# Cross attention and a mixture of experts on one core: bf16 slot tables, packed expert numbers, and two scatter buffers in turn

## What is computed

```python
logits = h @ router_w                                   # 8 experts, h: 1024 tokens x 128
probs = jax.nn.softmax(logits, axis=-1)
topv, topi = jax.lax.top_k(probs, TOPK)                  # TOPK = 2
topv = topv / jnp.sum(topv, axis=-1, keepdims=True)
weights = jnp.sum(jax.nn.one_hot(topi, E, dtype=h.dtype) * topv[..., None], axis=-2)
gate = jnp.einsum('bsd,edm->bsem', h, w_gate)            # m = 448
up = jnp.einsum('bsd,edm->bsem', h, w_up)
act = jax.nn.silu(gate) * up * weights[..., None]
moe = jnp.einsum('bsem,emd->bsd', act, w_down)
return x + moe
```

## Time and profile before

| | |
|---|---|
| time, median of 3 runs | 635.01 us (633.67 to 635.02) |
| the profiled execution's own time | 633.75 us |
| its span | 631.8 us |
| PE busy | 518.7 us, 82% of the span |
| DVE / ACT / POOL busy | 431.9 / 373.0 / 372.3 us |
| `mixture` begins | 483.6 us after the span's start |

### The profile page before, as it was taken

One profiled execution on the slowest core, in us unless ns is written; L12 is line 12 of the kernel. 1 busy time (PEld: TensorE's weight loads), 2 busy tenths in 40 slices (PEclk: granted clock), 3 DMA queues, 4 the chain that ended last, 5 costly groups with the idle time before them and its releaser, 6 DMA issues. The chain is left out here.

```text
span 631.8 us, 11030 instructions
## 1 busy us (share of the span) xinstructions
PE 518.7 (82%) x3275; PEld 407.3 (64%) x3275; DVE 431.9 (68%) x967; ACT 373.0 (59%) x968; POOL 372.3 (59%) x661
## 2 busy tenths in 40 slices
PE   5899899999899898999988647998986463999920
PEld 4567678777677676787766535665554463899920
DVE  5748877886888687978589526998984440577621
ACT  4548767877667766777677416898883200444400
POOL 1527966776777775787676556366965401565431
PEclk9789999999999999999999866999998555899975
DMA  8200010000100000000000011002220100011103
GB/s 298 66 1 1 2 34 2 1 2 2 35 0 2 2 1 1 1 2 2 2 0 2 2 49 47 2 1 89 88 89 18 33 0 18 29 48 39 35 21 108
DMA packets 17018, 18.49 MB, mean 29 GB/s; under 512 B 3041, under 2 KB 14305, under 8 KB 16961
## 3 DMA queue, kind: packets, MB, share of 16 engines
q1 hardware_dynamic: 15024, 14.71, 7.5%
q0 software_dynamic: 1472, 3.02, 1.5%
q10 hardware_dynamic: 464, 0.07, 0.1%
HBM read 15.23 MB, written 2.56 MB: 28 GB/s over the span
## 5 line engine op out<-in xcount | busy, mean ns | idle before, releaser
L1168 POOL TENSOR_SCALAR attn_probs<-attn_probs,rinv 128x512 f32<-128x512 f32 x128 | 90.4, 719 | 20.4 <-DVE rinv L1025 20.3
L860 ACT ACTIVATE attn_probs<-bank,bias 128x512 f32<-128x512 f32 x128 | 87.3, 687 | 13.6 <-DVE bias L1018 13.6
L1034 DVE TENSOR_TENSOR pT_lo<-bank,pT_hi 128x512 fp32r<-128x512 f32 x128 | 86.8, 680 | 7.4 <-ACT pT_hi L878 5.8
L690 PE MATMUL bank<-ident,attn_probs 128*128 128x128 f32 x512 | 78.4, 282 | 14.0 <-POOL attn_probs L1168 11.3
L1010 DVE TENSOR_REDUCE neg_max<-bank 128x1 f32<-128x512 f32 x128 | 83.9, 676 | 4.0 <-PE bank L673 4.0
L690 PEld LDWEIGHTS bank<-ident,attn_probs 128*128 128x128 f32 x512 | 56.3, 142 | 41.3 <-POOL attn_probs L1168 26.0
L878 ACT ACTIVATE pT_hi<-bank 128x512 fp32r<-128x512 f32 x128 | 74.2, 595 | 8.9 <-PE bank L690 8.0
L722 PE MATMUL bank<-pT_hi,vals 128*128 128x256 f32 x256 | 66.3, 291 | 2.2 <-DVE pT_lo L1034 1.4
L722 PE MATMUL bank<-pT_lo,vals 128*128 128x256 f32 x256 | 64.2, 283 | 0.0
L722 PEld LDWEIGHTS bank<-pT_hi,vals 128*128 128x128 f32 x256 | 48.8, 191 | 4.8 <-DVE pT_lo L1034 2.0
L1161 POOL TENSOR_TENSOR total<-row_sum,e 128x2 f32<-128x2 f32 x64 | 15.0, 234 | 62.3 <-ACT e L867 59.4
(11 more groups left out here) (312 smaller groups left out, 1490.0 us busy)
## 6 DMA issues: line engine op xcount, KB each, us to landing
ctx_raw<-in_ctx_T SPq DMA_DIRECT2D x4, 512.0 KB, 3.5
gu_raw<-in_L_ffn_w_gate SPq DMA_DIRECT2D x4, 448.0 KB, 3.5
gu_raw<-in_L_ffn_w_up SPq DMA_DIRECT2D x4, 448.0 KB, 4.3
wkv_raw<-in_L_xattn_Wkv SPq DMA_DIRECT2D x3, 512.0 KB, 8.9
dn_raw<-in_L_ffn_w_down SPq DMA_DIRECT2D x8, 192.0 KB, 4.2
y_in<-y_rows SPq DMA_DIRECT2D x4, 256.0 KB, 3.7
wkv_raw<-in_L_xattn_Wkv SPq DMA_DIRECT2D x2, 256.0 KB, 6.0
wq_raw<-in_L_xattn_Wq SPq DMA_DIRECT2D x1, 512.0 KB, 6.2
```

The lines of the kernel that those rows point to most:

```text
L690: last = pe.transpose(t_bank[half][:, j * N + t * P:j * N + (t + 1) * P], probs[:, g % 2, i, t, kt * P:(kt + 1) * P], k.ident[:, :])
L860: act.activation(probs[:, g % 2, i, t, :], score_bank(G, i)[:, :], ACT.Exp, bias=bias[:, t, h:h + 1], scale=X_SCALE, accum_out=row_sum[:, ...
L1034: dve.tensor_tensor(pT_lo[:, i, 2 * half:2 * half + 2, :], t_bank[half][:, :].rearrange("p (j n) -> p j n", j=2), f(pT_hi[:, i, 2 * half:2 ...
L1168: pool.tensor_scalar(probs[:, g % 2, i, t, :], probs[:, g % 2, i, t, :], rinv[:, t, h:h + 1], 1.0, ALU.mult, ALU.mult).then_inc(p_norm_s, 1)
```

## The change

The code of the attentions, of `fetch_pair` and of `split_pair` is the same. In `mixture`:

- The tables `chosen`, `in_tile`, `row_in`, `in_lane`, `share_in` become bf16, and so do the constants `earlier`, `ones`, `lanes`, which ACT casts from `slots` into `slots_b` as its first work in the stage. Numbers that bf16 doesn't hold are cut: `row_in` has two columns sets, a group number of 1 to 16 (`turns`) and the partition number (`row`), and a share is cut by POOL into three bf16 parts.
- The expert numbers of 8 tiles are packed into one number in base 8, so that PE reads 3 numbers instead of 23. The number of a tile is got back by a shift and a mask on PE's registers.
- The products of the shares stand behind gate and up of tile 0, and DVE, not ACT, makes `slot_share`.
- There are two buffers `y_rows0` and `y_rows1`. DVE fills `zeros` (128 x 2048) at the start of the stage and SP stores it to both, 1 MB each. Tile i scatters to buffer i % 2 and waits for the scatter of tile i-2. At the end all rows of both are read (4 DMAs of 512 KB) and added.
- The row of a pair is now 16 p + 2 t + j (partition p, tile t, choice j), so that what one partition reads or stores in DRAM is contiguous.

Its core as a diff:

```diff
+PACK = 8
+PACKS = -(-SLOT_TILES // PACK)
@@ sync
             sp.dma_start(k.slots[:, :], dram["slot_consts"]).then_inc(slots_in, 16)
+            sp.wait_ge(zeros_s, 1)
+            for a in range(COPIES):
+                sp.dma_start(y_rows[a][0:CHOICES * TOK, :].rearrange("(p t) d -> p (t d)", p=P), zeros[:, :]).then_inc(cleared, 16)
...
-            sp.wait_ge(scattered, 16 * SLOT_TILES)
+            for a in range(COPIES):
+                a = (SLOT_TILES + a) % COPIES
+                sp.wait_ge(scattered[a], 16 * len(range(a, SLOT_TILES, COPIES)))
+                for c in range(CH):
+                    sp.dma_start(y_in[:, a, 4 * c:4 * c + 4, :, :], y_rows[a][0:CHOICES * TOK, :]
+                                 .rearrange("(p t j) d -> p t j d", p=P, j=CHOICES)[:, 4 * c:4 * c + 4, :, :]).then_inc(y_back[a * CH + c], 16)
@@ tensor
-            pe.wait_ge(slots_in, 16)
+            pe.wait_ge(route_act, CAST_ACT)
...
-            pe.wait_ge(route_dve, SHARE_DVE)
-            for n in range(ROWS):
-                last = pe.matmul(share_bank, in_lane[:, n, :], share_in[:, n, :], start=n == 0, stop=n == ROWS - 1)
-            last.then_inc(route_ps, 1)
             pe.wait_ge(route_dve, EXPERT_DVE)
-            experts = [pe.value_load(expert[0:1, i:i + 1], min_val=0, max_val=E - 1) for i in range(SLOT_TILES)]
+            packs = [pe.value_load(packed[0:1, i:i + 1], min_val=0, max_val=E ** PACK - 1) for i in range(PACKS)]
+            experts = [(packs[i // PACK] >> (3 * (i % PACK))) & (E - 1) for i in range(SLOT_TILES)]
@@ the loop of PE
                     gate_up(i)
+                if i == 0:
+                    shares()
@@ scalar
+            act.wait_ge(slots_in, 16)
+            act.activation(k.slots_b[:, :], k.slots[:, 0:3 * P], ACT.Copy).then_inc(route_act, 1)
             for i in range(2):
                 act.wait_ge(route_ps, AOT_PS + i)
@@ gpsimd, scatter(i)
-                if i >= 1:
-                    pool.wait_ge(scattered, 16 * i)
-                pool.indirect_dma_start(y_rows, bass.IndirectOffsetOnAxis(y_at[:, i:i + 1], 0), y_row[:, i % RING, :], None)\
-                    .then_inc(scattered, 16)
+                if i < COPIES:
+                    pool.wait_ge(cleared, COPIES * 16)
+                else:
+                    pool.wait_ge(scattered[i % COPIES], 16 * (i // COPIES))
+                pool.indirect_dma_start(y_rows[i % COPIES], bass.IndirectOffsetOnAxis(y_at[:, i:i + 1], 0), y_row[:, i % RING, :], None)\
+                    .then_inc(scattered[i % COPIES], 16)
@@ vector
+            dve.memset(zeros[:, :], 0.0).then_inc(zeros_s, 1)
...
-            link(dve.tensor_scalar(y_at[:, :], row_bank, slot_const(k, "spare"), None, ALU.add))
-            dve.tensor_scalar(h_at[:, :], y_at[:, :], TOK - 1, None, ALU.bitwise_and).then_inc(route_dve, 1)
+            link(dve.tensor_scalar(unfilled[:, :], row_bank[:, 0, :], 0.0, slot_const(k, "spare"), ALU.is_equal, ALU.mult))
+            link(dve.scalar_tensor_tensor(row_of[:, :], row_bank[:, 1, :], float(CHOICES * TT), unfilled[:, :], ALU.mult, ALU.add))
+            link(dve.scalar_tensor_tensor(y_at[:, :], row_bank[:, 0, :], -1.0, row_of[:, :], ALU.add, ALU.add))
+            dve.tensor_scalar(h_at[:, :], y_at[:, :], 1, TOK - 1, ALU.logical_shift_right, ALU.bitwise_and).then_inc(route_dve, 1)
```

More of the change, by code:

```diff
@@ L1737, in _ @@
                 output_copy(s - 1)
-SLOT_CONSTS = {"earlier": P, "ones": P, "lanes": P, "filled": E, "lower": E * E, "tiles": SLOT_TILES, "starts": SLOT_TILES, "spare": 1,
-               "rows": CHOICES * TT}
+PACK = 8
+PACKS = -(-SLOT_TILES // PACK)
+SLOT_CONSTS = {"earlier": P, "ones": P, "lanes": P, "filled": E, "lower": E * E, "tiles": PACKS * PACK, "digits": PACKS * PACK,
+               "starts": SLOT_TILES, "spare": 1, "row": 1, "turns": CHOICES * TT}
 def slot_const(k, name):
@@ L1783, in mixture @@
         RING = 4
-        TURNS = 3
+        TURNS, PARTS = 3, 3
         h_rows = nc.dram_tensor("h_rows", (TOK, D), F32).ap()
-        y_rows = nc.dram_tensor("y_rows", (CHOICES * TOK + P, D), F32).ap()
+        COPIES = 2
+        y_rows = [nc.dram_tensor(f"y_rows{a}", (CHOICES * TOK + P, D), F32).ap() for a in range(COPIES)]
+        zeros = sb("zeros", [P, TT * CHOICES * D])
         k.slots = sb("slots", [P, sum(SLOT_CONSTS.values())])
+        k.slots_b = sb("slots_b", [P, 3 * P], BF16)
+        earlier, ones, lanes = (k.slots_b[:, n * P:(n + 1) * P] for n in range(3))
         x2, h2, base = sb("x2", [P, TT, D]), sb("h2", [P, TT, D]), sb("base", [P, TT, D])
@@ L1808, in mixture @@
         warm = sb("warm", [P, 1])
[L1809 removed]
+        y_in, total, res = sb("y_in", [P, COPIES, TT, CHOICES, D]), sq, aoT[:, :].rearrange("p (t d) -> p t d", d=D)
         banks = [bank(f"mix_bank{i}") for i in range(8)]
@@ L1888, in _, with shares @@
                     pe.wait_ge(route_dve, LANE_DVE + n // 4)
-                last = pe.matmul(row_bank, in_lane[:, n, :], row_in[:, n, :], start=n == 0, stop=n == ROWS - 1)
-            last.then_inc(route_ps, 1)
-            pe.wait_ge(route_dve, SHARE_DVE)
-            for n in range(ROWS):
-                last = pe.matmul(share_bank, in_lane[:, n, :], share_in[:, n, :], start=n == 0, stop=n == ROWS - 1)
+                last = pe.matmul(row_bank, in_lane[:, n, :], row_in[:, n, :, :], start=n == 0, stop=n == ROWS - 1)
             last.then_inc(route_ps, 1)
             pe.wait_ge(route_dve, EXPERT_DVE)
-            experts = [pe.value_load(expert[0:1, i:i + 1], min_val=0, max_val=E - 1) for i in range(SLOT_TILES)]
+            packs = [pe.value_load(packed[0:1, i:i + 1], min_val=0, max_val=E ** PACK - 1) for i in range(PACKS)]
+            experts = [(packs[i // PACK] >> (3 * (i % PACK))) & (E - 1) for i in range(SLOT_TILES)]
+            def shares():
+                pe.wait_ge(route_dve, SHARE_DVE)
+                for n in range(ROWS):
+                    last = pe.matmul(share_bank, in_lane[:, n, :], share_in[:, n, :, :], start=n == 0, stop=n == ROWS - 1)
+                last.then_inc(route_ps, 1)
             def turn_rows(i):
                 pe.wait_ge(gathered[i % RING], 16 * (i // RING + 1))
-                if i == 0:
-                    pe.wait_ge(route_act, SHARE_ACT)
-                else:
+                if i >= 1:
                     pe.wait_ge(hT_lo_s, i)
@@ L2021, in _ @@
             pool.tensor_tensor(share[:, 1, :], odds[:, :], share[:, 0, :], ALU.mult).then_inc(route_pool, 1)
+            pool.wait_ge(route_pool, SHARE_POOL)
+            whole = share[:, :, :].rearrange("p j t -> p (j t)")
+            for a in range(PARTS):
+                pool.tensor_scalar(share_part[:, a, :], whole if a == 0 else share_rest[:, :], 1.0, 1.0, ALU.mult, ALU.mult)\
+                    .then_inc(route_pool, 1)
+                if a + 1 < PARTS:
+                    pool.wait_ge(route_pool, PART_POOL + 2 * a)
+                    pool.tensor_tensor(share_rest[:, :], whole if a == 0 else share_rest[:, :], share_part[:, a, :], ALU.subtract)\
+                        .then_inc(route_pool, 1)
+                    pool.wait_ge(route_pool, PART_POOL + 2 * a + 1)
             def gather(i):
@@ new lines, in _ @@
+            link(dve.tensor_tensor(passed[:, :, :], passed[:, :, :],
+                                   slot_const(k, "digits").unsqueeze(2).broadcast_to([P, PACKS * PACK, E - 1]), ALU.mult))
+            link(dve.tensor_reduce(packed_f[:, :], passed[:, :, :].rearrange("p (g i) e -> p g (i e)", i=PACK), AX_X, ALU.add))
+            dve.tensor_copy(packed[:, :], packed_f[:, :]).then_inc(route_dve, 1)
+            dve.wait_ge(route_pool, PART_POOL + 2 * PARTS - 2)
+            for a in range(PARTS):
+                last = dve.tensor_tensor(share_in[:, :, a, :], in_tile[:, :, :],
+                                         share_part[:, a, :].unsqueeze(2).broadcast_to([P, ROWS, SLOT_TILES]), ALU.mult)
@@ L2242, in shape_constants @@
         "lower": rows(np.tril(np.ones((E, E)), -1)),
-        "tiles": rows(np.arange(SLOT_TILES)),
+        "tiles": rows(np.arange(PACKS * PACK)),
+        "digits": rows(np.tile(float(E) ** np.arange(PACK), PACKS)),
         "starts": rows(P * np.arange(SLOT_TILES)),
-        "spare": CHOICES * TOK + row,
-        "rows": TOK * np.repeat(np.arange(CHOICES), TT)[None, :] + P * np.tile(np.arange(TT), CHOICES)[None, :] + row - CHOICES * TOK,
+        "spare": CHOICES * TOK + 1 + row,
+        "row": row,
+        "turns": rows(CHOICES * np.tile(np.arange(TT), CHOICES) + np.repeat(np.arange(CHOICES), TT) + 1),
     }
```

89 lines of the change are left out of this document (47 added, 42 removed).

## The result

The changed kernel took 604.42 us, the median of four runs (604.24 to 605.90), against 635.01 for the kernel before in the same comparison (four runs, 633.67 to 635.85): the ratio is 0.9525 (0.9503 to 0.9547). The forecast was 603.0, the range 599 to 608. The profiled execution took 604.47, with a span of 602.3.

A forecast was written before the change was run, and what follows sets the result against it. Waits and PE at half clock bound the start, PE alone the loop, then scatters 3.03 us apart. 633.75 - 18.45 + 0.95 - 0.7 - 13.3 = 602.25 for the profiled execution; named 603.0, range 599 to 608.

The forecast's parts named there:

- Start: Start of the mixture: ACT waits for the load of `slots` and casts it before `aoT`, so all behind is 3.3 us late.
- Queue products: PE's queue products in the routing: bf16 needs 9 passes instead of 18, each with a shorter weight load; -2.85 us.
- Row products: PE's products on `in_lane`: 16 passes instead of 32, so PE ends 0.8 us after the last piece; -4.25 us.
- Indices: Ahead of `h_at`: three linked operations instead of one, two more of 0.28 us; +0.55 us.
- Reads: Ahead of the first tile: PE reads 3 numbers at 0.5 us each, so the gather ends last; first turning -18.45 in all.
- Shares: 16 share products behind gate and up of tile 0: 0.9 us at full clock, 1.8 at half; +0.95 us.
- Registers: Two more register operations a tile in PE's loop, hidden by its backlog of products: 0, upper end 2.1 us.
- No scatter wait: Seven tiles late in the loop take 18.83 us at 2.69 each instead of 19.51, without waits for scatters; -0.7 us.
- Tail: Behind the last gate and up: last scatter lands 13.5 us earlier, doubled reading back costs 0.2; -13.3 us.

The follow-up runs named there:

- the later cast: The changed kernel with ACT's cast of the constants moved behind its copies of h2T, ahead of odds: 601.06 us, ratio to the kernel before 0.9464.

## Why the prediction was right, step by step

The account of the stage held: the first tile starts when the first gather lands, PE alone bounds the loop, and the tail shrinks because scatters go to two buffers. Terms that were off partly cancelled, which was luck.

Set back one at a time, the reads, the second buffer and the bf16 tables moved the end of the stage by 12.7, 11.3 and 12.8 us. That is 36.8, against the 31.1 won and the 3.1 that the early cast costs. They needn't add up: 4 us of the reads were hidden under the share products before, and 1.7 of the 12.8 is the later load.

- **Start, forecast +3.3, measured +3.50.** The load landed in 3.77 instead of 3.6, the cast took 0.52 instead of 0.45. Shown by the later cast: with it `aoT` comes 3.04 earlier.
- **Queue products, -2.85 and -3.50.** Mis-sized: I halved the weight load with the width. It fell to about a third, and the products stood 0.04 apart where I had assumed 0.11.
- **Row products, -4.25 and -4.72.** The added operation on `row_in` took 0.22 instead of 0.3, and PE's result was there 0.42 behind the last piece (514.82 to 515.24) instead of 0.8. `in_lane` stayed at 0.62 a piece (2.49 for four): the narrower type alone gave nothing. By the Trainium skill ("VectorE: DVE Perf Modes", What auto-detection actually checks) two-operand operations double their rate only if every tensor is 16-bit and read with a step of one. The trace agrees: the second operand here is repeated along the row.
- **Indices, +0.55 and +0.43.**
- **Reads.** The prediction's "11.4 us / 23 = 0.5 each" failed: 0.66 each. The forecast survived because three reads (517.3 to 519.4) still end before the gather lands near 519.7, 0.3 later; I had put 0.9 between them, and a little dearer read would have moved the first turning. The turning came 2.78 behind the gather, forecast 2.85. The 0.50 I had read off a wait that began late. The Trainium skill ("DMA: Bandwidth & Descriptors", Latency and other measured facts) gives some 600 ns as the floor of one load; the 0.66 measured here agrees with it, and my 0.50 lay below.
- **Shares, +0.95.** Their 16 products take 0.96 in the chain, still at half clock (0.50 from 519.8 to 526), and 0.06 apart. I had 1.8 for them at half clock and got to 0.95 by a clock that would rise earlier; the number was right by luck. Note that these products have 69 columns and the queue products, 0.04 apart, 64 down to 8, so in bf16 the wider products stood further apart, while the fp32 passes of before stood 0.21 apart with 64 down to 8 columns and 0.22 with 23.
- **Registers, 0.** PE was busy 35.00 of 35. No gap, no price.
- **No scatter wait, -0.7.** The loop changed by +0.19. That fits 0.96 for the shares and some -0.7 for the stalls, and the last tiles, 2.97, 2.68, 2.84 and 2.96 apart before, now stand 2.68 or less apart. But the parts weren't measured apart, the moment at which the clock rises is in the sum too, and the kernel with one buffer had no such stalls either.
- **Tail, -13.3 and -11.78.** The mis-sized term. The last scatter started 7.53 behind the last gate and up, forecast 7.3. It landed 2.66 later where I took 2.23; beside the reads of the other buffer it is slower (2.23 again with one buffer). And the last 1 MB came 6.97 after that landing, not 6.2. From the first issue at 589.16, 2.1 MB took 8.93; less 1.9 at the start that is 0.30 MB/us, between the 0.26 of before and my 0.36. 0.2 + 0.4 (landing) + 0.8 make 1.4 of the 1.5 missing. What the contiguous rows gave wasn't tried by itself: with one buffer 1 MB was back 5.2 after the first issue, in two DMAs, where before it took 5.97 in four.

For the profiled execution the sum gave 602.25, and it took 604.47: 0.4 of the 2.2 is in the stage, 1.6 in the untouched attentions, 0.2 outside the span.

## What to carry to other kernels

Before pricing an "issue" on the chain, look at the sequencer's own instructions of that line: they may have begun beneath work that was still queued, and then the visible part is no price. Where a cast or a load is put first in an engine's program, its wait is paid by everything queued behind it. This one cost 3.0 us until it was moved to where its result is needed. And when scatters wait for each other only because they share a buffer, a second buffer frees them, but reading it back takes some of this away: here 13.5 became 11.3. A forecast that rests on one of two waits ending last should say by how much; here it was 0.3 us.

## What the runs showed that I had not expected

- The narrower weight load at half clock takes 0.116 instead of 0.333, more than the width explains, and products of 64 down to 8 columns follow each other at 0.04.
- The clock does not rise at a fixed distance from the first turning. 3.2 to 6.2 us behind it were granted 0.50 in the changed kernel, 0.77 with the later cast, 0.68 with the zeros stored later and 0.84 with one buffer, all with the same order of work on PE. From the first turning to the last gate and up these four took 61.1, 60.4, 60.7 and 60.3, so a gain of less than 1 us in the loop can't be read from one trace.
- A scatter that lands beside a read-back takes longer: 2.23 without one, in the kernels with one buffer; 2.6 to 2.9 in the five traces where SP issued the first read 0.70 to 0.72 us behind the scatter's start; 3.9 to 4.2 in the three where it came 0.18 to 0.47 behind (4.22 in the fp32 kernel). Why isn't shown, and within the loop, with no read-back near, some scatters took 3 to 4 us as well.
